# Weight quarters, weight loads and early feed-forward products move to other slots of a transformer block kernel on one Trainium2 core

## Chip, core and metric

The kernel runs on one core of a Trainium2 chip. The metric is the device time of one execution in microseconds (us); lower is better.

## What is computed

A transformer block over 16 sequences of 256 rows of 256 numbers, all fp32: self attention, cross attention against a context of 192 numbers per row, and a gated feed-forward. Cut to what matters:

```python
D_MODEL, D_COND, N_HEADS, D_HEAD = 256, 192, 16, 64
D_ATTN, D_FF = N_HEADS * D_HEAD, 4 * D_MODEL
def _attention(xq, xkv, wq, wk, wv, wo, bo):
    q, k, v = xq @ wq, xkv @ wk, xkv @ wv          # split into 16 heads of 64
    attn = softmax(q k^T * D_HEAD ** -0.5)
    return (attn v) @ wo + bo
h = _layernorm(x, ln1_g, ln1_b)
x = _attention(h, h, sa_wq, sa_wk, sa_wv, sa_wo, sa_bo) + x
h = _layernorm(x, ln2_g, ln2_b)
x = _attention(h, cond_emb, ca_wq, ca_wk, ca_wv, ca_wo, ca_bo) + x
h = _layernorm(x, ln3_g, ln3_b)
p = h @ ff_w1 + ff_b1
a, gate = p[..., :D_FF], p[..., D_FF:]
x = (a * gelu(gate)) @ ff_w2 + ff_b2 + x
```

## The kernel before

Every fp32 product is made of three rounded ones (high by high, high by low, low by high), so most operands exist as a pair high and low, and some engine splits them.

**Slots.** Attention is a software pipeline, written out by hand, of 256 slots (ATT), one for each pair of heads of each sequence: slots 0 to 127 are self attention, 128 to 255 cross attention, eight (PAIRS) for each sequence. In slot c, TensorE (PE) makes the scores of pair c (tile S, L428/L429), a projection of queries and keys for a later pair (QKB), part of a projection of values (VB), the output product of pair c-4 (WOP, L577), the transposes of the probabilities of c-1 (PTB, L539), and probabilities by values of c-2 (PVB, L597). VectorE (DVE) finds the row maxima (NM), splits QKB and the probabilities (PL), adds halves; ScalarE (ACT) does the exponentials (PT) and copies out of PSUM; GpSimd (POOL) splits values (VR), divides and splits the outputs (ON, then OT, in that order behind everything else of its slot) and splits weights. Each engine works its slots strictly in order.

**Projections.** For slots 0 to 31 (OLD) and for the last eight (LAST = 248 on) a pair is projected alone, three slots ahead (AHEAD): `pe_project`, L508. In between one product serves two sequences, keys and queries in turns, seven slots ahead (LEAD): `pe_project_both`, L526. Where both fall into one slot (c = 25 to 28, called late), the lone one comes behind the transposes. There is one bank QKB: each product waits until DVE has split the one before (L843 or L851). As the lone ones of the end start at c = 245, slots 241 to 244 have no projection, and neither have 253 to 255.

**Copies.** SyncE (SP) walks the same slots. In each turn it issues four copies of a pair's queries and keys (RX from QKS, L630 and L632, needed by the scores), one store and two loads of the softmax denominators, and what else is due: rows, x, weights. The denominators' load waits for POOL's product ON of two pairs earlier (L1498).

**Weights.** The cross-attention weights and then the feed-forward ones are staged in six chunks each: SP loads a chunk of 512 KB into STG in a sequence's first slot (pair 0). POOL splits it in four quarters (`pool_split_w`: L1019, L1021, and for the query chunks a scaling, L1017) into a ring of two places (SPL) in the pairs QUARTERS, 1, 2, 5 and 6; SP stores each quarter to DRAM one turn later (`store_split`, L1538). Split k waits until store k-2 has landed. The chunks are staged in sequences 4 to 9 and 17 to 22. Near slot 112 to 129, and again near slot 240 to 257, SP loads them into WA: for each pair of heads four transfers of 128 KB (`load_pair`, two in each of two turns), and for the values' chunks four of 256 KB per half (`load_four`).

**Feed-forward.** It has 64 steps, eight for each of eight chunks of rows: a first product (12 matmuls of 512 columns, L1184), Gelu on ACT, product and split on DVE, a second product (12 of 256 columns, L1202). The rows of the first chunk are prepared during slots 240 to 254, and steps 0 to 3 are woven into PE's slots 256 to 259.

## Time and profile before

| | us |
|---|---|
| median of 3 runs (lowest to highest) | 1746.31 (1742.96 to 1747.38) |
| the profiled execution's own time | 1743.33 |
| its span | 1741.5 |
| mean granted clock of TensorE | 0.997 |
| PE busy | 1701.8 (98%) |
| DVE, ACT, POOL busy | 1406.2, 1236.6, 1086.2 |

The span runs from the first to the last instruction of the profiled execution; its own time is 1.8 us longer. PE counts as busy from a matmul's start to its modelled end, so that short waits do not show in its share. A window is a stretch of the span, counted from its start.

### The profile page before, as it was taken

To read this page: it belongs to the slowest core of one execution; us is meant where nothing else is said; L and a number is where in the kernel's file an instruction comes from. 1 tells how busy PE (TensorE), PEld (TensorE's weight loads), DVE (VectorE), ACT (ScalarE), POOL (GpSimd) and SP (SyncE) were. 2 spreads that over 40 slices of the span, in tenths; PEclk is the share of its full clock that TensorE was granted. 3 is DMA by queue.
4 is the path that set the end of the run, shared out by engine and by line. 5 is a ranking of instruction groups with operands and counts; after the bars stand their busy time and mean duration, and the time that the engine had idled before them with its cause. 6 is when DMAs were issued, how large, how long until landed. Compare 5 with 4: busy or idle time off the path is not lost.

```text
span 1741.5 us, 39097 instructions
## 1 busy us (share of the span) xinstructions
PE 1701.8 (98%) x11712; PEld 1564.2 (90%) x11712; DVE 1406.2 (81%) x2964; ACT 1236.6 (71%) x3370; POOL 1086.2 (62%) x1812
## 2 busy tenths in 40 slices
PE   9999999999999999999999999999999999999999
PEld 8998898989999999889888899999999888888888
DVE  8897788888888888788888888888888877656664
ACT  7887777878888888778778788888888776222222
POOL 7775577767766666688777777777776555222211
PEclk9999999999999999999999999999999999999999
DMA  7775577778766677887777788776666776211210
GB/s 217 182 184 144 155 201 189 195 194 213 194 179 156 157 176 194 214 208 189 197 202 200 206 207 205 175 184 169 166 168 161 177 200 159 73 49 61 66 45 25
DMA packets 321234, 288.92 MB, mean 166 GB/s; under 512 B 104064, under 2 KB 281344, under 8 KB 321024
## 3 DMA queue, kind: packets, MB, share of 16 engines
q1 hardware_dynamic: 267232, 273.29, 60.4%
q10 hardware_dynamic: 53792, 13.12, 3.5%
q8 instruction: 96, 1.57, 0.4%
q14 instruction: 114, 0.93, 0.2%
HBM read 82.98 MB, written 37.49 MB: 69 GB/s over the span
## 4 chain that ended last, share of the span: by engine, by line
PE 64%; SPq 17%; issue 4%; DMA 4%; POOL 4%; DVE 3%; ACT 3%; ACTq 0%; POOLq 0%; DVEq 0%
PE QKB L526 9%; PE PVB L597 9%; PE PTB L539 8%; PE WOP L577 6%; PE VB L461 5%; PE PTB L1184 5%; PE S L1184 5%; SPq L632 5%; SPq L630 4%; PE S L428 4%; PE S L429 4%; SPq L1502 4%; PE QKB L1202 3%; PE VB L1202 3%; PE QKB L508 2%
## 5 line engine op out<-in xcount | busy, mean ns | idle before, releaser
L734 ACT ACTIVATE PT<-S,NM 128x256 f32<-128x256 f32 x1024 | 471.1, 472 | 193.2 <-DVE NM L862 192.5
L837 DVE TENSOR_TENSOR PL<-PTB,PH 128x512 fp32r<-128x512 f32 x512 | 350.8, 686 | 147.8 <-ACT PH L761 125.3
L1075 POOL TENSOR_TENSOR ON<-ON,RB 128x256 f32<-128x256 f32 x256 | 187.9, 734 | 283.9 <-DVE ON L882 261.4
L862 DVE TENSOR_REDUCE NM<-S 128x2 f32<-128x512 f32 x512 | 326.4, 679 | 0.4
L761 ACT ACTIVATE PH<-PTB 128x1024 fp32r<-128x1024 f32 x256 | 265.5, 1037 | 41.3 <-PE PTB L539 39.7
L539 PE MATMUL PTB<-IDN,PT 128*128 128x128 f32 x2048 | 271.3, 274 | 5.2 <-DVE PL L837 5.1
L428 PE MATMUL S<-RX 128*128 128x256 f32 x1012 | 254.9, 284 | 2.4 <-DMA RX<-QKS 1.9
L429 PE MATMUL S<-RX 128*128 128x256 f32 x1012 | 254.0, 283 | 0.0
L577 PEld LDWEIGHTS WOP<-WO,OT 128*128 128x128 f32 x1536 | 216.1, 190 | 38.7 <-POOL OT L1080 19.2
L526 PE MATMUL QKB<-HT,WA 128*128 128x512 f32 x936 | 242.4, 394 | 2.3 <-DVE QKS L843 2.0
L539 PEld LDWEIGHTS PTB<-IDN,PT 128*128 128x128 f32 x2048 | 230.0, 140 | 10.8 <-DVE PL L837 10.2
L577 PE MATMUL WOP<-WO,OT 128*128 128x256 f32 x1536 | 225.9, 283 | 13.9 <-POOL OT L1080 13.6
L882 DVE TENSOR_TENSOR ON<-PVB,ON 64x256 f32<-64x256 f32 x512 | 213.4, 417 | 3.5
L710 ACT ACTIVATE ON<-PVB 64x256 f32<-64x256 f32 x512 | 193.9, 379 | 21.9 <-PE PVB L597 5.7
L734 ACT ACTIVATION_READ_ACCUMULATOR PT<-S,NM 128x1 f32 x1024 | 207.5, 203 | 0.0
L1080 POOL TENSOR_TENSOR OT<-ON,OT 128x256 fp32r<-128x256 f32 x256 | 191.6, 748 | 20.5
L1056 POOL TENSOR_TENSOR VR<-VF,VR 128x256 fp32r<-128x256 f32 x256 | 189.2, 739 | 20.5
L428 PEld LDWEIGHTS S<-RX 128*128 128x128 f32 x1012 | 194.1, 192 | 3.8 <-DMA RX<-QKS 3.8
L429 PEld LDWEIGHTS S<-RX 128*128 128x128 f32 x1012 | 194.6, 192 | 0.0
L526 PEld LDWEIGHTS QKB<-HT,WA 128*128 128x128 f32 x936 | 165.8, 189 | 30.8 <-DVE QKS L843 2.8
L597 PE MATMUL PVB<-PH,VR 128*128 128x256 f32 x1024 | 184.1, 301 | 6.3 <-issue 5.7
L851 DVE TENSOR_TENSOR QKS<-QKB,QKS 128x512 fp32r<-128x512 f32 x216 | 149.4, 692 | 22.6 <-ACT QKS L690 9.2
(151 smaller groups left out, 2941.9 us busy)
## 6 DMA issues: line engine op xcount, KB each, us to landing
RX<-QKS SPq DMA_DIRECT2D x506, 192.0 KB, 2.9
RX<-QKS SPq DMA_DIRECT2D x506, 128.0 KB, 2.9
RB<-denominators SPq DMA_DIRECT2D x512, 64.0 KB, 2.7
weights<-SPL SPq DMA_DIRECT2D x48, 256.0 KB, 3.3
out_dram<-XR SPq DMA_DIRECT2D x32, 256.0 KB, 3.7
WA<-weights SPq DMA_DIRECT2D x64, 128.0 KB, 2.7
rows<-XN SPq DMA_DIRECT2D x24, 256.0 KB, 2.6
rows<-HF SPq DMA_DIRECT2D x23, 256.0 KB, 2.7
```

The costliest lines, as they stand in the source:

```text
L428: e.matmul(o, q, RX[:, c % 2, i, K1, :], start=True, stop=False)
L429: last = e.matmul(o, q, RX[:, c % 2, i, K2, :], start=False, stop=True)
L526: last = e.matmul(QKB[:, :], w[:, p * P:(p + 1) * P], act, start=i == 0, stop=i == len(passes) - 1)
L539: last = e.transpose(PTB[:, i, kt * S + qt * P:kt * S + (qt + 1) * P], PT[:, s % 2, q0:q0 + P], IDN[:, :])
L577: last = e.matmul(WOP[:, t * D:(t + 1) * D], OT[:, op, t * P:(t + 1) * P], WO[:, p, wp, :], start=begins(s) and t == 0 and j == 0, stop=en ...
L597: last = e.matmul(PVB[:, i * S:(i + 1) * S], VR[:, s // 2 % 2, kt, s % 2, i * P:(i + 1) * P], part[:, first:first + S], start=i == 0 and j ...
L710: last = e.activation(ON[OWN[i], s % 2, :], PVB[OTHER[i], i * S:(i + 1) * S], ACT.Copy)
L734: last = e.activation(PT[:, c % 2, j * S:(j + 1) * S], S1[:, i, qt * S:(qt + 1) * S], ACT.Exp, bias=NM[:, j:j + 1], accum_out=DEN[:, c % 2 ...
L761: e.activation(PH[:, s % 2, :], PTB[:, :, :].rearrange("p i n -> p (i n)"), ACT.Copy) \
L837: e.tensor_tensor(PL[:, cols], PTB[:, i, :], PH[:, s % 2, cols].bitcast(F32), ALU.subtract).then_inc(a.dve_pl, 1)
L862: e.tensor_reduce(NM[:, i * TT:(i + 1) * TT], S1[:, i, :].rearrange("p (t s) -> p t s", t=TT), AX.X, ALU.max, negate=True).then_inc(a.dve_ ...
L882: last = e.tensor_tensor(on, PVB[OWN[i], i * S:(i + 1) * S], on, ALU.add)
```

## The change

- POOL's quarters of the cross weights are split in the pairs 3, 4, 5 and 6 of sequences 4 to 9 (they were in 1, 2, 5, 6). Those of the feed-forward weights are split two to a sequence, in the pairs 5 and 6 (HALVES), over sequences 17 to 28, with a staging load in every second sequence. The scaling of the query weights (L1017) goes; the norm's gain and bias get the factor, once, on ACT.
- The stored quarters are counted by two semaphores, one for each place of SPL.
- `load_pair` is one transfer of 512 KB for a pair of heads, in one turn (there were four of 128 KB in two turns). `load_four` is two transfers of 512 KB per half, in every second turn (there were four of 256 KB in four turns).
- In the late slots 25 to 28 the values' product stands ahead of the joint projection.
- The last eight pairs are projected seven slots ahead (c = 241 to 248) and take other places in QKS. In slots 249 to 254 the six first products of feed-forward steps 0 to 2 (EARLY = 3) are made in QKB by the new `pe_raw`, and ACT copies them to SBUF (`act_copy_raw`, one copy each).
- The preparation of the first rows moves ten slots ahead (FFN_START = ATT - 10), its split rows lie in HT, and the later steps' splits in QKS. PE's slots 256 to 259 are woven with first products 3, 4 and 5 and second products 0 and 1.

```diff
-CROSS_LOADS = 4
+VALUE_LOADS = 2
+EARLY = 3
+RAWS = 2 * EARLY
+FFN_START = ATT - 10
 SPLIT = 4
 PIECES = ((0, 0), (1, 0), (2, 0), (0, 1), (1, 1), (0, 2), (1, 2), (2, 1), (2, 2), (0, 3), (1, 3), (2, 3))
-QUARTERS = (1, 2, 5, 6)
+QUARTERS = (3, 4, 5, 6)
+HALVES = (5, 6)
...
+    if last_alone(k):
+        return (7, 1, 2, 0, 3, 4, 5, 6)[k - LAST]
...
-            late = 0 < c < DIRECT or joint(c + LEAD) and alone(c + AHEAD)
+            late = 0 < c < DIRECT or joint(c + LEAD) and first_alone(c + AHEAD)
+            if late and joint(c + LEAD):
+                pe_value_turn(e, c)
             if joint(c + LEAD):
                 pe_project_both(e, c + LEAD)
-            if alone(c + AHEAD) and not late:
+            if first_alone(c + AHEAD) and not late:
                 pe_project(e, c + AHEAD)
-
-            if 0 <= c < ATT:
+            if last_alone(c + LEAD):
+                pe_project(e, c + LEAD)
+            if ATT <= c + LEAD < ATT + RAWS:
+                pe_raw(e, c + LEAD - ATT)
+
+            if 0 <= c < ATT and not (late and joint(c + LEAD)):
...
+            if n == B:
+                e.wait_ge(s_gain, 1)
...
-            if k > DIRECT + 1:
+            if k >= LAST:
+                held = max(m for m in range(DIRECT, k) if unit(m) == unit(k))
+                e.wait_ge(d_dup[held % 2], 16 * COPIES * copied(held))
...
             if k > 1:
-                e.wait_ge(d_ws, 16 * (k - 1))
-            if done == 0 and n < KD:
-                e.tensor_scalar(STG[:, cols], STG[:, cols], SCALE, None, ALU.mult).then_inc(s_sc, 1)
-                e.wait_ge(s_sc, k + 1)
+                e.wait_ge(d_ws[k % 2], 16 * (k // 2))
...
-            if pair in QUARTERS and B + 1 <= seq <= B + NCH:
-                pool_split_w(e, seq - B - 1, 3 + NCH + seq - B, QUARTERS.index(pair), NCH)
+            if pair in HALVES and B + 1 <= seq <= B + 2 * NCH:
+                n, half = divmod(seq - B - 1, 2)
+                pool_split_w(e, n, 4 + NCH + n, 2 * half + HALVES.index(pair), NCH)
...
-        FH = HT[:, 0, :, :, :, :].rearrange("p a k x s -> p (a k x s)") \
-            .rearrange("p (r a s) -> p r a s", r=2, a=2)
+        FH = QKF.rearrange("p (r a s) -> p r a s", r=2, a=2)
+        SPF = SPL[:, :, :, :].rearrange("p r a n -> p r (a n)").bitcast(F32)
...
+        def pe_raw(e, n):
+
+            c, g = divmod(n, 2)
+            if n == 0:
+                e.wait_ge(a.dve_lo, ATT)
+                e.wait_ge(fs.s_ht, KD)
+            else:
+                e.wait_ge(fs.act_raw, n)
+            if g == 0:
+                e.wait_ge(d_wq[c % 2], 16 * (PAIRS // 2 + c // 2 + 1))
+            i = 0
+            for k in range(KD):
+                for wp, ap in ((0, 0), (0, 1), (1, 0)):
+                    last = e.matmul(QKB[:, :], w1(k, wp, g * FF + c * P), rounded(0, ap, k), start=i == 0, stop=i == 5)
+                    i += 1
+            last.then_inc(fs.pe_raw, 1)
+
+        def act_copy_raw(e, n):
+
+            e.wait_ge(fs.pe_raw, n + 1)
+            e.activation(RAW[n], QKB[:, :], ACT.Copy).then_inc(fs.act_raw, 1)
...
-            if sl.has(c):
+            if sl.has(c) and firsts:
...
-            if sl.has(c - 1):
+            if sl.has(c - 1) and seconds:
...
-                sl.wait(e, fs.pe_f1, c + 1)
+                if c < EARLY:
+                    e.wait_ge(fs.act_raw, 2 * c + 2)
+                else:
+                    e.wait_ge(fs.pe_f1, firsts(c) + 1)
...
+                e.activation(LNG[:, 1, :, :], LNG[:, 1, :, :], ACT.Copy, scale=SCALE).then_inc(s_gain, 1)
...
-            if sl.c == ATT - 3:
-                e.wait_ge(d_dup[0], 16 * COPIES * copied(LAST - 2))
-                e.wait_ge(d_dup[1], 16 * COPIES * copied(LAST - 1))
+            if sl.c == FFN_START - 3:
+                e.wait_ge(a.pe_qk, products_of(2 * B - 4))
                 pool_ffn_hi(e, 0)
-            if sl.c == ATT - 2:
+            if sl.c == FFN_START - 2:
                 pool_ffn_hi(e, 1)
                 pool_ffn_low(e, 0)
+            if sl.c == FFN_START - 1:
                 pool_ffn_low(e, 1)
...
+            def load_pair(phase, p):
 
                 cols = slice(p * P, (p + 1) * P)
-                for n in chunks:
-                    e.dma_start(WA[:, n, :, cols].bitcast(F32), WS[phase, :, n, :, cols]).then_inc(d_wq[p % 2], 16)
+                e.dma_start(WA[:, 0:4, :, cols].bitcast(F32), WS[phase, :, 0:4, :, cols]).then_inc(d_wq[p % 2], 16)
 
             def load_four(phase, g, n):
 
-                cols = slice((2 * g + n % 2) * QW, (2 * g + n % 2 + 1) * QW)
-                e.dma_start(WA[:, 4 + n // 2, :, cols].bitcast(F32), WS[phase, :, 4 + n // 2, :, cols]) \
-                    .then_inc(d_wv[g], 16)
+                cols = slice(g * HC, (g + 1) * HC)
+                e.dma_start(WA[:, 4 + n, :, cols].bitcast(F32), WS[phase, :, 4 + n, :, cols]).then_inc(d_wv[g], 16)
 
...
-                if pair in QUARTERS and B + 1 <= seq <= B + NCH:
-                    store_split(QTR * (NCH + seq - B - 1) + QUARTERS.index(pair))
+                if pair in HALVES and B + 1 <= seq <= B + 2 * NCH:
+                    store_split(QTR * NCH + 2 * (seq - B - 1) + HALVES.index(pair))
...
+                        if phase and g:
+                            k = ATT - QUAD + i
+                            at = k - LEAD + 2
+                            freed = nth_alone(k) + 1
+                        else:
+                            j = first - 2 * PAIRS + 2 * p + 1
+                            at = j - LEAD + 3
+                            freed = nth_joint(j) + 1
+                        if c == at:
+                            await_stored(phase)
+                            e.wait_ge(a.pe_qk, freed)
+                            if p > 1:
+                                e.wait_ge(d_wq[p % 2], 16 * (PAIRS // 2 * phase + p // 2))
+                            load_pair(phase, p)
                     for g in range(2):
                         four = first - 2 * PAIRS + PAIRS * g + QUAD
...
-                        for n in range(4):
-                            if c == four + 2 + n:
-                                e.wait_ge(d_ws, 16 * QTR * NCH * (phase + 1))
+                        for n in range(2):
+                            if c == four + 2 + 2 * n:
+                                await_stored(phase)
                                 e.wait_ge(a.pe_v, tiles(four) + 2)
                                 load_four(phase, g, n)
 
...
-                if pair == 0 and B + 1 <= seq <= B + NCH:
-                    if seq == B + 1:
+                if pair == 0 and B + 1 <= seq <= B + 2 * NCH and (seq - B) % 2:
+                    n = (seq - B - 1) // 2
+                    if n == 0:
                         e.wait_ge(s_ow, 2 * PAIRS)
                     else:
-                        e.wait_ge(s_pw, QTR * (NCH + seq - B - 1))
-                    stage_ffn(seq - B - 1)
...
-            for j in range(4):
-                pe_ffn(e, Slot(j, FU, 2))
-                pe_slot(e, Slot(ATT + j, ATT))
-            ffn(e, pe_ffn, 4)
+            pe_slot(e, Slot(ATT, ATT))
+            pe_ffn(e, Slot(EARLY, FU, 2), seconds=False)
+            pe_slot(e, Slot(ATT + 1, ATT))
+            pe_ffn(e, Slot(1, FU, 2), firsts=False)
+            pe_slot(e, Slot(ATT + 2, ATT))
+            pe_ffn(e, Slot(EARLY + 1, FU, 2), seconds=False)
+            pe_ffn(e, Slot(2, FU, 2), firsts=False)
+            pe_slot(e, Slot(ATT + 3, ATT))
+            pe_ffn(e, Slot(EARLY + 2, FU, 2), seconds=False)
+            for c in range(3, EARLY + 3):
+                pe_ffn(e, Slot(c, FU, 2), firsts=False)
+            ffn(e, pe_ffn, EARLY + 3)
```

## Rows read from the trace of the kernel before

**Rows 1.** Windows of the span: busy time (matmuls) of each engine, granted clock, DMA share.
```profile
480.00:640.00 160.00, 160.00 (x1122) 149.05 (x1121) 138.40 (x296) 129.81 (x368) 103.78 (x176) 1.00 0.65 163
...
1060.00:1376.00 316.00, 314.79 (x2212) 291.38 (x2211) 278.74 (x589) 262.73 (x742) 218.26 (x371) 1.00 0.70 174
...
210.00:400.00 190.00, 184.80 (x1284) 170.30 (x1283) 157.26 (x335) 149.25 (x419) 140.41 (x237) 1.00 0.75 194
690.00:800.00 110.00, 106.79 (x728) 96.25 (x727) 91.35 (x193) 86.54 (x245) 79.97 (x139) 1.00 0.81 206
840.00:1060.00 220.00, 210.16 (x1443) 192.36 (x1442) 184.22 (x391) 171.54 (x483) 164.36 (x286) 0.98 0.79 203
1376.00:1464.00 88.00, 79.61 (x592) 71.76 (x591) 68.35 (x153) 65.92 (x191) 48.67 (x81) 1.00 0.75 194
...
855.50:858.90 3.40, 3.40 (x19) 3.40 (x18) 0.39 (x1) 1.96 (x4) 3.24 (x6) 0.50 0.81 190
```

**Rows 2.** PE's groups of matmuls between 1376 and 1464 us (busy, mean ns, idle before).
```profile
L539 PE MATMUL PTB<-IDN,PT 128*128 128x128 f32 x128 | 18.8, 277 | 4.7 <-DVE PL L837 4.6
...
L461 PE MATMUL VB<-WA,CT 128*128 128x512 f32 x31 | 9.3, 395 | 0.0
L508 PE MATMUL QKB<-HT,WA 128*128 128x256 f32 x48 | 7.1, 283 | 0.0
```

**Rows 3.** Waits between 840 and 1060 us: total us, times, longest.
```profile
POOL SPL L1019 <- DMA STG<-in_L_xattn_ff_w_dram: 21.3, 5, 5.4
...
PEld WOP L577 <- POOL OT L1080: 11.5, 7, 3.0
```

**Rows 4.** Timeline of POOL: a feed-forward quarter whose chunk lands late.
```profile
850.43 0.40 POOL L1019 CAST SPL<-STG 128x256 fp32r<-128x256 f32 x1 [4.87 <-DMA STG<-in_L_xattn_ff_w_dram]
```

**Rows 5.** Timeline of PE: the output product in the same slot.
```profile
854.34 0.97 PE L577 MATMUL WOP<-WO,OT 128*128 128x256 f32 x6 [2.04 <-POOL OT L1080]
```

**Rows 6.** Timeline of POOL: a quarter split without a wait, in a pair 5.
```profile
418.34 0.40 POOL L1019 CAST SPL<-STG 128x256 fp32r<-128x256 f32 x1
```

**Rows 7.** Timeline of SP: stores of the quarters of rows 6 and of rows 4.
```profile
427.33 0.59 SPq L1538 DMA_DIRECT2D weights<-SPL  x1
...
857.52 0.61 SPq L1538 DMA_DIRECT2D weights<-SPL  x1
```

**Rows 8.** DMA issues, whole span: size of one, median us to landing.
```profile
RX<-QKS SPq DMA_DIRECT2D x506, 192.0 KB, 2.9
...
weights<-SPL SPq DMA_DIRECT2D x48, 256.0 KB, 3.3
...
STG<-in_L_xattn_ff_w_dram SPq DMA_DIRECT2D x6, 512.0 KB, 5.8
```

**Rows 9.** Timeline of SP during the cross-weight loads, about one turn.
```profile
717.43 1.09 SPq L1545 DMA_DIRECT2D WA<-weights  x2
718.62 0.42 SPq L1550 DMA_DIRECT2D WA<-weights  x1
...
724.07 0.54 SPq L1545 DMA_DIRECT2D WA<-weights  x1
```

**Rows 10.** Waits between 690 and 800 us.
```profile
PEld S L428 <- DMA RX<-QKS: 2.8, 6, 1.1
```

**Rows 11.** Timeline of SP in a stretch without weight transfers.
```profile
1127.79 0.62 SPq L632 DMA_DIRECT2D RX<-QKS  x1
1129.25 1.10 SPq L1502 DMA_DIRECT2D RB<-denominators  x2
```

**Rows 12.** Timeline of PE: first scores of the pair whose last copy is in rows 11.
```profile
1134.94 0.28 PE L428 MATMUL S<-RX 128*128 128x256 f32 x1
```

**Rows 13.** Timeline of PE in late slot 26: the joint projection, then the lone one.
```profile
163.18 1.66 PE L526 MATMUL QKB<-HT,WA 128*128 128x512 f32 x6 [0.50 <-DVE QKS L843]
...
167.16 1.10 PE L508 MATMUL QKB<-HT,WA 128*128 128x256 f32 x7
```

**Rows 14.** Timeline of DVE in the same slot: the joint projection's split.
```profile
166.42 0.69 DVE L851 TENSOR_TENSOR QKS<-QKB,QKS 128x512 fp32r<-128x512 f32 x1
```

More of the change, by code:

```diff
@@ L68, in alone, with first_alone, last_alone @@
     return 0 <= k < OLD or LAST <= k < ATT
+def first_alone(k):
+    return 0 <= k < OLD
+def last_alone(k):
+    return LAST <= k < ATT
 def joint(j):
@@ L286, in block_kernel @@
         d_wst = sem("d_wst")
-        d_ws = sem("d_ws")
+        d_ws = [sem(f"d_ws{n}") for n in range(2)]
         d_wq = [sem(f"d_wq{n}") for n in range(2)]
@@ L700, in act_slot @@
             c = sl.c
-            late = joint(c + LEAD) and alone(c + AHEAD)
+            late = joint(c + LEAD) and first_alone(c + AHEAD)
             if sl.has(c - 3):
@@ L739, in act_slot @@
                 act_copy_qk(e, 2)
-            elif alone(c + AHEAD) and not late and not -1 <= c < DIRECT - 1:
+            elif first_alone(c + AHEAD) and not late and not -1 <= c < DIRECT - 1:
                 act_copy_qk(e, c + AHEAD)
@@ L855, in dve_slot @@
             c = sl.c
-            late = joint(c + LEAD) and alone(c + AHEAD)
+            late = joint(c + LEAD) and first_alone(c + AHEAD)
             if sl.has(c):
@@ L900, in dve_slot @@
                 dve_split_qk(e, 2)
-            elif alone(c + AHEAD) and not late and not -1 <= c < DIRECT - 1:
+            elif first_alone(c + AHEAD) and not late and not -1 <= c < DIRECT - 1:
                 dve_split_qk(e, c + AHEAD)
@@ L1094, in __init__ @@
             def __init__(self):
+                self.pe_raw = sem("pe_raw_f")
+                self.act_raw = sem("act_raw_f")
                 self.pe_f1 = sem("pe_f1_f")
@@ L1129, in gates, with firsts @@
         def gates(c, g):
-            return (QKB, VB)[g][:, :] if c == 0 else AG[c % 2][:, g, :]
+            return RAW[2 * c + g] if c < EARLY else AG[c % 2][:, g, :]
+        def firsts(c):
+            return c - EARLY
         ROWS = (XN[:, :], HF[:, :])
@@ L1221, in act_ffn_round @@
             if chunk > 1:
-                e.wait_ge(fs.pe_f1, PAIRS * (chunk - 1))
+                e.wait_ge(fs.pe_f1, firsts(PAIRS * (chunk - 1)))
             e.activation(rounded(chunk, 0, k), ROWS[k], ACT.Identity, bias=LNG[:, 2, 1, k:k + 1],
@@ L1538, in store_split, with await_stored @@
                 e.dma_start(WS[n // NCH, :, n % NCH, :, quarter * QW:(quarter + 1) * QW],
[L1539 to L1541 removed]
+                            SPL[:, k % 2, :, :].bitcast(F32)).then_inc(d_ws[k % 2], 16)
+            def await_stored(phase):
+                for done in d_ws:
+                    e.wait_ge(done, 16 * QTR // 2 * NCH * (phase + 1))
+            def load_pair(phase, p):
                 cols = slice(p * P, (p + 1) * P)
[L1544 to L1545 removed]
+                e.dma_start(WA[:, 0:4, :, cols].bitcast(F32), WS[phase, :, 0:4, :, cols]).then_inc(d_wq[p % 2], 16)
             def load_four(phase, g, n):
[L1549 to L1551 removed]
+                cols = slice(g * HC, (g + 1) * HC)
+                e.dma_start(WA[:, 4 + n, :, cols].bitcast(F32), WS[phase, :, 4 + n, :, cols]).then_inc(d_wv[g], 16)
             def fill_weights(c):
@@ L1562, in fill_weights @@
                         g, i = divmod(p, QUAD)
-                        for half in range(2):
-                            if phase and g:
-                                k = ATT - QUAD + i
-                                at = k
-                                freed = nth_alone(k) + 1
-                            else:
-                                j = first - 2 * PAIRS + 2 * p + 1
-                                at = j - LEAD + 3 + half
-                                freed = nth_joint(j) + 1
-                            if c == at:
-                                e.wait_ge(d_ws, 16 * QTR * NCH * (phase + 1))
-                                e.wait_ge(a.pe_qk, freed)
-                                if p > 1 and half == 0:
-                                    e.wait_ge(d_wq[p % 2], 16 * CROSS_LOADS * (PAIRS // 2 * phase + p // 2))
-                                load_pair(phase, p, 2 * half, 2 * half + 1)
+                        if phase and g:
[12 more added lines that the diff above has]
+                            load_pair(phase, p)
                     for g in range(2):
                         four = first - 2 * PAIRS + PAIRS * g + QUAD
-                        for n in range(4):
-                            if c == four + 2 + n:
-                                e.wait_ge(d_ws, 16 * QTR * NCH * (phase + 1))
+                        for n in range(2):
+                            if c == four + 2 + 2 * n:
+                                await_stored(phase)
                                 e.wait_ge(a.pe_v, tiles(four) + 2)
```

76 lines of the change are left out of this document (43 added, 33 removed).

## The prediction

> **What bounds the kernel now.** I read the windows of the span first. TensorE (PE) counts as busy in nearly every microsecond, so the question is only where it works slower than it can. Its matmuls can be counted: a stretch that nothing disturbs gives a pace, and what another stretch takes beyond that pace was lost there, short waits under the modelled ends of matmuls included [rows 1].
>
> The self-attention slots from 480 to 640 us take 160 us for 1122 matmuls, 0.1426 us each; the cross-attention slots from 1060 to 1376 us take 316 us for 2212, 0.1429 us each. A slot has 38 or 39 matmuls, so it takes 5.43 us (cross) or 5.56 us (self). Four stretches are slower [rows 1]:
>
> - 210 to 400 us (cross weights split on POOL): 1284 x 0.1426 = 183.1, so 6.9 us lost.
> - 690 to 800 us (cross weights loaded by SP): 728 x 0.1429 = 104.0, so 6.0 us lost.
> - 840 to 1060 us (feed-forward weights split): 1443 x 0.1429 = 206.1, so 13.9 us lost.
> - 1376 to 1464 us (the last slots). The mix differs, so I go by columns. A cross slot has 10,752 (22 matmuls of 256, 8 of 512, 8 of 128), in 5.43 us: 1,980 columns a microsecond. The 592 matmuls here are 128 of 128 columns, 32 of 512 (31 values, one feed-forward) and 432 of 256 (among them 88 of the eight lone projections, 48 of which have a row) [rows 2]: 143,360 columns, 72.4 us. So 15.6 us of 88 are lost.
>
> Together 42.4 us. The waits then name the culprits. Between 840 and 1060 us POOL waits 21.3 us in five pieces for a staged chunk, and PE waits for OT [rows 3]. The timeline shows one piece: POOL stands 4.87 us at the first quarter, and in that slot PE stands 2.04 us at the output product [rows 4, 5]. So a late POOL of up to 4.87 - 2.04 = 2.8 us is absorbed. Behind this idle piece the granted clock is 0.50 for 3.4 us, its lower level of 1.2 GHz: 1.7 us more [rows 1]. In the last slots PE's idle time before the transposes is DVE's PL [rows 2]: four slots and then three have no projection between the scores and the transposes, and without that cover DVE's maxima and split are seen.
>
> **The change part by part.**
>
> *Quarters in other pairs.* The chunk is issued in pair 0 and lands 5.8 us later (median) [rows 8], about one slot. POOL asks for it in pair 3 (three slots, 16 us) or pair 5, so this wait goes: 13.9 us in the feed-forward part, and the 6.9 us of the self part, where L1017 goes too. POOL's own work stays under a slot: it is busy 164 of 220 us with the quarters [rows 1]. There is a new wait, however. In the self part four quarters now follow in four slots, and split k needs the store of k-2 landed. From a split's start to its store's issue the timeline shows 427.33 - 418.34 = 9.0 us, and a store lands 3.3 us later [rows 6, 7, 8]: 12.3 us against two slots, 11.1 us. So POOL will stand some 1.2 us in pairs 5 and 6. Behind it in its slot are ON and OT, which the output product waits for, but 2.8 us are absorbed. And the wait limits itself: with POOL late, the issue came 857.52 - 850.43 = 7.1 us behind the split [rows 4, 7], because SP is then paced by POOL's own ON; 10.4 us in all. PE should see nothing. Bounds: 0 to 6.9 us; I take 6.5 us for the self part. The feed-forward quarters have a whole sequence between k and k+2. I leave 0.9 us for their later neighbours and take 13.0 us (bounds 9.3, if a third stays as another wait, to 13.9). The new wait for the gain's factor is for work done a hundred slots earlier: nothing.
>
> *Fewer weight transfers.* In the loading stretch one turn of SP takes 724.07 - 717.43 = 6.64 us, more than a slot of 5.43; 1.7 us of it are three weight transfers [rows 9]. The queue is the bound there, and PE's scores wait for late copies [rows 10]. Without them a turn has 0.8 us left, from 1128.41 to 1129.25 [rows 11], so its work is some 4.6 us. With pairs in odd turns and fours in even ones there is now at most one transfer in a turn, 0.55 us if the larger one costs as much to issue [rows 9]: 5.2 us, just under a slot. Rows and x transfers come on top in some turns, and the bytes are the same. So the stretch is nearly, not wholly, freed: 4.5 us of 6.0 (bounds: a loss of 13, see the rivals, to 6.0). In the last slots the same transfers are fewer too; that is in the next term but one.
>
> The Trainium skill (DMA: Bandwidth & Descriptors, Anatomy of one DMA) puts a DMA at about 2.0 us plus its bytes by 436 GB/s, given for the GpSimd path; for 512 KB that would be 3.2 us, and merging four transfers would cost almost nothing. The trace doesn't agree under this load: 5.8 us for a staged chunk of that size [rows 8]. By the page this term would be the whole 6.0 us, by the row the 4.5 us taken.
>
> *Values first in the late slots.* In slot 26 the joint projection waits 0.50 us for QKB, and the values ahead of it would fill that [rows 13]. But the lone projection starts at 167.16, 0.05 us after DVE ends the joint split at 166.42 + 0.69 [rows 13, 14]. DVE comes to this split through the maxima and ACT's exponentials of the same scores, which the order of the values doesn't touch. So the wait moves from the joint to the lone projection. I take 0; bounds 0 and 3 x 0.50 = 1.5 us.
>
> *The last slots.* Fourteen slots (241 to 254) get a projection or a raw product each, so PE's slots are full and the covers are back. Nothing is added for PE: the 36 matmuls of the raw products are taken from the feed-forward steps. The copies of a pair's queries and keys no longer hang on a projection three slots ahead; normally they have 1134.94 - 1127.79 - 2.9 = 4.2 us to spare [rows 8, 11, 12]. ACT makes six PSUM copies more, in slots where it had none of QKB to copy; DVE has no split for them. The first rows' preparation falls into slots 230 to 245, where DVE is 88% busy [rows 1], as it is while any sequence is prepared, and no other sequence is. PE's slot 255 and the four behind it stay thin: scores 255, then only outputs and transposes before the first products. Of 15.6 us I leave 3.0 for both. That is 12.6 us (bounds 6, if DVE sets half of the slots, to 15.6).
>
> Sum: 6.5 + 13.0 + 4.5 + 0 + 12.6 = 36.6 us. Against the profiled execution's own 1743.33 that is 1706.7 us. That execution lies 3.0 us under the median of the runs, so the same saving from the median gives 1709.7; I forecast 1708 us.
>
> **The rivals.**
>
> *The large load holds the copies back.* A transfer of 512 KB takes 5.8 us where one of 192 KB takes 2.9 [rows 8], and the copies of the next turn follow it in the queue. The delay of 2.9 us is under the spare 4.2 us, which speaks against; but the spare is thin where the queue is full. If each of the twelve large loads of the first phase costs the longest wait seen there, 1.1 us [rows 10], that is 13 us, and the 4.5 us aren't had: 1724 us. The Trainium skill (same page, Queues, rings and completion order) says that the descriptors of a queue are consumed in ring order, which is this rival's mechanism; no row here separates it from the issue time.
>
> *The end stays bound by DVE.* Then it gives 6 us and not 12.6: 1713 us. For it: PL ends PE's waits there. Against: the slots before 1376 us have the same DVE work and run at full pace.
>
> *The store's landing becomes the wait, and it is slower.* It decides once the lag from split to landing passes 11.1 + 2.8 = 13.9 us. At a POOL wait as long as that of rows 4, lag 16 us, each of the twelve splits in pairs 5 and 6 of the self part idles PE 2.04 us [rows 5] and draws 1.7 us of half clock [rows 1]: 12 x 3.74 = 45 us more, 1752 us, slower. Against: 12.3 and 10.4 us measured. At a lag of 15 us it is 1.1 us each, too short for the clock to fall: 13 us, 1720 us.
>
> *The waits only change names.* POOL and SP are freed, but ACT's or DVE's order sets the same pace: no change, 1746 us. Against: two long stretches without these waits run at 0.143 us a matmul.
>
> **How the numbers follow.** Forecast as such 0.70 (1699 to 1713), DVE-bound end 0.12, held copies 0.08, store's landing in its milder form 0.03 and its slower form 0.03, names only 0.04. The low end is all terms in full and the 1.5 us: 1743.3 - 42.4 - 1.5 = 1699. The high end takes in the first rival, 1724. A measurement of this kernel tells 0.3%, some 5 us. Faster 0.93, same 0.04, slower 0.03.
>
> **What would show it.** Right: no wait of POOL's quarters for the staged chunks; short waits, 1 to 2 us, for the stores in pairs 5 and 6 of sequences 4 to 9, and no PE wait for OT behind them; granted clock 1.00 throughout; from 840 to 1060 us some 1540 matmuls instead of 1443; SP's turns with weights under 5.5 us; in the late slots the 0.50 us moved to the lone projection; slots 241 to 254 of 5.4 us. Wrong: PE waiting for RX in slots 110 to 130, POOL waits above 2.8 us, or slots near 240 at 5.8 us and more with PE waiting for PL.

## The result, and the profile after

The changed kernel takes 1714.82 us (median of 4 runs, 1713.36 to 1716.02), the kernel before 1744.63 (4 runs beside them, 1742.15 to 1747.38). The ratio is 0.9828, with a 95% interval of 0.9809 to 0.9847. The forecast was 1708, range 1699 to 1724. The span went from 1741.5 to 1713.0 us, 28.5 us less, where the sum of the prediction had 36.6.

Which part gave what can be read from the starts of the slots. In each trace I take from PE's timeline where the transposes of pair n begin (PTB<-IDN,PT, L539 before, L555 after), and subtract. PE makes the transposes of pair n in its slot n+1; a stretch "slots 32 to 118", here and in the experiments, runs from the transposes of pair 32 to those of pair 118.

| stretch | before, from to | after, from to | saved | predicted |
|---|---|---|---|---|
| start to slot 32 (values first) | 0, 212.93 | 0, 213.03 | -0.1 | 0 |
| slots 32 to 118 (self quarters) | 212.93, 699.42 | 213.03, 691.98 | 7.5 | 6.5 |
| 118 to 136 (loads) | 699.42, 803.77 | 691.98, 790.04 | 6.3 | 4.5 |
| 136 to 200 (feed-forward quarters) | 803.77, 1165.40 | 790.04, 1138.12 | 13.5 | 13.0 |
| 200 to 224 | 1165.40, 1295.89 | 1138.12, 1268.66 | 0.0 | 0 |
| 224 to the end (last slots) | 1295.89, 1741.54 | 1268.66, 1712.98 | 1.3 | 12.6 |

Four terms came as large as predicted or a little larger. The largest but one, 12.6 us, gave 1.3. First the windows of the changed kernel; the columns are as in [rows 1] (window, length, PE, PEld, DVE, ACT, POOL, granted clock, DMA share, GB/s).

```profile
210.00:400.00 190.00, 190.00 (x1332) 177.05 (x1331) 162.65 (x348) 154.96 (x434) 139.69 (x239) 1.00 0.77 200
690.00:800.00 110.00, 109.34 (x768) 101.23 (x767) 96.75 (x208) 90.86 (x257) 86.34 (x149) 1.00 0.81 207
840.00:1060.00 220.00, 218.93 (x1543) 202.62 (x1541) 195.93 (x415) 183.50 (x515) 166.23 (x285) 1.00 0.79 200
...
1438.80:1442.10 3.30, 3.30 (x17) 3.26 (x15) 1.77 (x3) 1.16 (x2) 1.51 (x3) 0.50 0.48 168
1455.90:1459.20 3.30, 3.30 (x9) 2.52 (x9) 2.19 (x4) 0.00 (x0) 0.00 (x0) 0.50 0.44 137
```

The three long stretches now run at 0.1426, 0.1432 and 0.1426 us a matmul, the undisturbed pace of the two stretches in [rows 1]; before they had 1284, 728 and 1443 matmuls in the same lengths. The two short windows are new: the granted clock falls to 0.50 in PE's slot 256 and again behind slot 259, for 3.4 us each; each window lies within one such piece. Between 690 and 800 us PE no longer waits for RX [rows 10]. Between 210 and 400 us this is all that POOL's quarters wait for (total us, times, longest):

```profile
POOL SPL L1049 <- DMA weights<-SPL: 4.5, 6, 1.1
```

The wait for a staged chunk [rows 3, 4] is gone here and between 840 and 1060 us, and in its place stand six short ones for the stores. Over all 24 quarters of the self part (to 480 us) there are eight, 7.8 us in all, the longest 1.9. No PE wait for OT stands behind them.

In the late slots the timeline of PE shows the 0.50 us of [rows 13] gone and a wait in front of the lone projection instead:

```profile
163.32 1.60 PE L542 MATMUL QKB<-HT,WA 128*128 128x512 f32 x6
...
167.27 0.98 PE L524 MATMUL QKB<-HT,WA 128*128 128x256 f32 x6 [0.77 <-DVE QKS L882]
```

The tail is where the gain is missing. PE's timeline of the changed kernel in slots 255 to 259:

```profile
1434.18 0.71 PE L619 MATMUL PVB<-PH,VR 128*128 128x256 f32 x4 [0.89 <-issue]
...
1437.75 0.95 PE L599 MATMUL WOP<-WO,OT 128*128 128x256 f32 x6 [2.38 <-DVE XR L969]
...
1438.54 1.69 PE L555 MATMUL PTB<-IDN,PT 128*128 128x128 f32 x8
...
1441.73 3.13 PE L1243 MATMUL S<-HT,WA 128*128 128x512 f32 x12
...
1455.64 0.65 PE L1243 MATMUL S<-HT,WA 128*128 128x512 f32 x1 [2.05 <-DVE PT L1372]
```

PE waits 2.38 us for DVE's sum before the output product of slot 256, 0.89 us at PVB of slot 255, and 2.05 us at the first products of feed-forward step 5 (L1243). Right behind each of the two longer waits comes one of the two half-clock pieces. DVE's timeline says what it was doing before it let PE go at 1455.64:

```profile
1440.26 0.75 DVE L1372 SCALAR_TENSOR_TENSOR PT<-SPL,B,PT 128x512 f32<-128x512 f32 x1 [1.89 <-PE PTB L555]
...
1449.40 0.75 DVE L1372 SCALAR_TENSOR_TENSOR PT<-XN,B,PT 128x512 f32<-128x512 f32 x1
1450.19 0.85 DVE L1376 CAST QKS<-PT 128x512 fp32r<-128x512 f32 x1
1451.07 0.77 DVE L1378 TENSOR_TENSOR QKS<-PT,QKS 128x512 fp32r<-128x512 f32 x1
1451.77 1.57 DVE L829 TENSOR_SCALAR XN<-XR,MV,RSTD 128x256 f32<-128x256 f32 x2
1453.26 1.55 DVE L829 TENSOR_SCALAR HF<-XR,MV,RSTD 128x256 f32<-128x256 f32 x2
1454.84 0.75 DVE L1372 SCALAR_TENSOR_TENSOR PT<-S,B,PT 128x512 f32<-128x512 f32 x1
...
1461.78 0.43 DVE L1376 CAST QKS<-PT 128x512 fp32r<-128x512 f32 x1 [3.62 <-PE VB L1264]
```

Without a gap it does the product and split of an early step (L1372, L1376, L1378, 2.4 us) and the normalization of the next chunk's rows (L829, 3.1 us) and only then the product that reads S (step 3's), which first product 5 waits for, as it is made in the same bank. DVE's timeline shows no gap from 1440.26 us, behind the transposes of pair 255, to 1458.16 us.

In the kernel before, the output product of slot 256 stands behind first product 0 and doesn't wait:

```profile
1463.90 1.55 PE L1184 MATMUL QKB<-QKS,WA 128*128 128x512 f32 x6
1465.29 1.52 PE L1184 MATMUL VB<-QKS,WA 128*128 128x512 f32 x6
1466.65 0.88 PE L577 MATMUL WOP<-WO,OT 128*128 128x256 f32 x6
```

### The profile page after: what moved, and what is told of

Its sections match the earlier page's. It is cut to its first block, busy times and chain, and to the rows that moved or that the text cites. A ratio compares the mean times of both kernels' runs of the same rounds, so it can differ in the third digit from the quotient of the medians.

```text
span 1713.0 us, 39030 instructions
## 1 busy us (share of the span) xinstructions
PE 1689.9 (99%) x11712; PEld 1563.7 (91%) x11712; DVE 1407.4 (82%) x2964; ACT 1239.4 (72%) x3377; POOL 1084.6 (63%) x1804
## 3 DMA queue, kind: packets, MB, share of 16 engines
q8 instruction: 96, 1.57, 0.4%
## 4 chain that ended last, share of the span: by engine, by line
PE 89%; SPq 3%; DVE 3%; ACT 2%; issue 2%; DMA 1%; POOL 0%; ACTq 0%; DVEq 0%; POOLq 0%
PE QKB L542 16%; PE PVB L619 13%; PE PTB L555 12%; PE WOP L599 9%; PE VB L477 8%; PE S L444 6%; PE S L445 6%; PE S L1243 5%; PE PTB L1243 5%; PE QKB L1264 3%; PE VB L1264 3%; PE QKB L524 2%; ACT PT L761 1%; SPq L656 1%; SPq L654 1%
## 5 line engine op out<-in xcount | busy, mean ns | idle before, releaser
L555 PE MATMUL PTB<-IDN,PT 128*128 128x128 f32 x2048 | 268.4, 273 | 0.3 <-DVE PL L868 0.2
L555 PEld LDWEIGHTS PTB<-IDN,PT 128*128 128x128 f32 x2048 | 229.9, 140 | 3.2 <-DVE PL L868 3.0
L619 PE MATMUL PVB<-PL,VR 128*128 128x256 f32 x1024 | 163.9, 282 | 0.0
```

What stands on the lines that cost most here:

```text
L555: last = e.transpose(PTB[:, i, kt * S + qt * P:kt * S + (qt + 1) * P], PT[:, s % 2, q0:q0 + P], IDN[:, :])
L619: last = e.matmul(PVB[:, i * S:(i + 1) * S], VR[:, s // 2 % 2, kt, s % 2, i * P:(i + 1) * P], part[:, first:first + S], start=i == 0 and j ...
```

## The experiments

Each was compared with the kernel before, run on the same chip; the chips differ between some experiments, so across them I compare ratios, and stretches of the traces. "Span" is that of the profiled execution.

**1. The quarters alone.** On the kernel before:

```diff
-QUARTERS = (1, 2, 5, 6)
+QUARTERS = (3, 4, 5, 6)
+HALVES = (5, 6)
...
-            if pair in QUARTERS and B + 1 <= seq <= B + NCH:
+            if pair in HALVES and B + 1 <= seq <= B + 2 * NCH:
```

with the staging in every second sequence, two store semaphores and the gain's factor on ACT, as in the change.

> The kernel before with the quarters' part alone: splits in pairs 3 to 6 of sequences 4 to 9 and in pairs 5 and 6 of sequences 17 to 28, two store semaphores, the factor in the norm's gain. Theory (POOL's wait for the staged chunk was all that this stretch lost): it keeps the 7.5 us and the 13.5 us that the changed kernel gained there, 21 us in all, so a ratio of 0.988, and TensorE's clock is granted in full. Rival (part of that gain needs SP's queue freed by the merged loads): at most 15 us, 0.991 or more.

Measured: 1724.74 us against 1742.72, ratio 0.9893 (0.9873 to 0.9913), span 1723.9. By slot starts 6.9 us are saved up to slot 118, and 18.7 up to slot 200 and 224. The loading stretch isn't helped (118 to 136 takes 105.5 us, 1.2 more than before), 136 to 200 gains 12.9, and 1.0 us is lost again from 224 on. The window of its feed-forward quarters stands at full pace already:

```profile
840.00:1060.00 220.00, 218.83 (x1536) 202.16 (x1534) 195.91 (x415) 182.14 (x515) 164.95 (x282) 1.00 0.79 199
```

So the two quarter terms hold, each by itself.

**2. The loads alone.** On the kernel before:

```diff
-            e.wait_ge(d_wq[p % 2], 16 * CROSS_LOADS * (p // 2 + 1))
+            e.wait_ge(d_wq[p % 2], 16 * (p // 2 + 1))
...
+            def load_pair(phase, p):
+                cols = slice(p * P, (p + 1) * P)
+                e.dma_start(WA[:, 0:4, :, cols].bitcast(F32), WS[phase, :, 0:4, :, cols]).then_inc(d_wq[p % 2], 16)
...
-                        for n in range(4):
-                            if c == four + 2 + n:
+                        for n in range(2):
+                            if c == four + 2 + 2 * n:
```

> The kernel before with the merged weight loads alone. Theory (SP's queue was the bound near slots 118 to 130): about 6 us gained there; in the last slots, where four of the large loads come in four turns running, copies land late and 1 to 3 us of it go again: ratio 0.997 to 0.998. Rival (the large load holds the copies back in the first phase too): no gain, 1.000 or more.

Measured: 1732.71 against 1742.72, ratio 0.9938 (0.9918 to 0.9959), span 1731.7. That is more than either theory gave it. Slots 118 to 136 take 97.5 us (before 104.4), 6.8 us less; 136 to 200 gain 2.8 and the stretch from 224 on 2.5. The stretch from the start to slot 96 is 2.2 us slower, and I have no cause for that. The larger loads don't hold the copies back in the first phase: between 690 and 800 us PE has no wait for RX.

```profile
690.00:800.00 110.00, 109.51 (x775) 101.80 (x773) 96.02 (x204) 91.02 (x257) 84.43 (x146) 1.00 0.84 214
840.00:1060.00 220.00, 211.29 (x1460) 191.54 (x1459) 188.36 (x397) 174.62 (x494) 167.78 (x291) 1.00 0.80 206
```

775 matmuls where there were 728: with the quarters untouched, the merged loads alone take away the whole of this stretch's loss. The second window keeps most of the quarters' loss (1460, not 1540).

**3. Quarters and loads, nothing early.** Both edits; no values first, no raw products, no rows prepared early.

> The changed kernel without its last part and without the values first: quarters and merged loads, but the old last slots, no early products, first rows prepared as before. Theory (the last slots gained only 1 to 2 us, as the two traces say when their ends are compared): 1716 us, ratio 0.984. Rival, the step as predicted (12.6 us gained by the early products and lost elsewhere): 1727 us, 0.990.

Measured: 1713.63 against 1742.72, ratio 0.9831 (0.9807 to 0.9854), span 1711.3. It is as good as the whole change. So the early feed-forward products bring nothing in total, and the last stretch can be compared between the two kernels with their loads alike. Windows of this kernel, from slot 224 to 239, from there to 255, and the 38.4 us behind:

```profile
1267.90:1348.70 80.80, 80.61 (x572) 75.01 (x571) 70.05 (x147) 67.28 (x192) 54.14 (x92) 1.00 0.71 179
1348.70:1436.90 88.20, 81.03 (x605) 73.82 (x604) 70.95 (x157) 68.03 (x193) 51.30 (x85) 1.00 0.74 196
1436.90:1475.30 38.40, 38.40 (x237) 34.47 (x236) 25.07 (x48) 11.05 (x18) 16.40 (x21) 1.00 0.15 47
```

The same three windows of the changed kernel:

```profile
1268.70:1351.40 82.70, 81.97 (x572) 75.09 (x571) 73.41 (x159) 67.01 (x192) 55.29 (x94) 1.00 0.69 178
1351.40:1438.50 87.10, 82.24 (x628) 78.22 (x627) 67.49 (x145) 71.33 (x199) 49.98 (x83) 1.00 0.80 197
1438.50:1477.00 38.50, 36.45 (x212) 32.69 (x211) 26.20 (x48) 10.95 (x18) 17.47 (x21) 0.91 0.13 44
```

- 224 to 239: 1.9 us longer for the same 572 matmuls; DVE has 12 instructions and 3.4 us more (the first rows' statistics and normalization). The 1.9 us come between the transposes of pairs 231 and 237; DVE has these instructions from pair 229 to pair 236, and those of sequence 31 before them, from 223 to 226.
- 239 to 255: 1.1 us shorter, although it holds net 24 matmuls of 512 columns more (36 raw ones less the 12 of the first product 0, which the other kernel has there), 5.5 us by the 2.75 us that twelve take on the timeline. So 6.6 us of waiting are gone: the cover works.
- 255 to the end: 274.44 against 274.43 us, although it has those 24 matmuls less. So 5.5 us are lost. In 38.5 us PE does 212 matmuls instead of 237, at a clock of 0.91.

In sum 0.9 us lost (444.32 us from slot 224 to the end, against 443.44). Against the kernel before, the merged loads and the quarters bring 2.2 us from slot 224 on, and the early products take 0.9 back: the 1.3 of the table.

**4. Joint projection first in the late slots,** as before, all else changed:

```diff
-            if late and joint(c + LEAD):
-                pe_value_turn(e, c)
...
-            if 0 <= c < ATT and not (late and joint(c + LEAD)):
+            if 0 <= c < ATT:
```

> The changed kernel with the joint projection ahead of the values again in slots 25 to 28. Theory (DVE's chain sets the lone projection): slot 32's transposes start within 0.2 us of the changed kernel's 213.03 us; the joint projection waits 0.50 us again and the lone one that much less. Rival (the order earns what it fills): 1.5 to 2.0 us later.

Measured, a single run: 1715.08 us, span 1713.3, slot 32 at 212.99 (changed kernel 213.03), and the joint projection waits 0.50 us again. The order of the two is worth nothing, in either direction.

This trace shows something else. PE has the same wait of 2.38 us before slot 256's output product, but the clock stays at 1.00 behind it; only one half-clock piece is left, at step 5, so that the mean over the same 38.5 us is 0.96:

```profile
1437.69 0.95 PE L597 MATMUL WOP<-WO,OT 128*128 128x256 f32 x6 [2.38 <-DVE XR L967]
...
1438.40:1476.90 38.50, 35.09 (x210) 31.02 (x209) 26.82 (x48) 10.98 (x18) 17.41 (x21) 0.96 0.14 44
```

From slot 255 to the end it takes 274.78 us all the same, where the changed kernel with both pieces takes 274.44.

**5. The last loads one turn apart.** In the last slots of the changed kernel the pair loads come in four SP turns running, with a value load in the same turn as one of them:

```profile
RX<-QKS SPq DMA_DIRECT2D x4, 192.0 KB, 4.7
RX<-QKS SPq DMA_DIRECT2D x5, 128.0 KB, 5.2
WA<-weights SPq DMA_DIRECT2D x4, 512.0 KB, 9.5
```

These are DMA issues between 1395 and 1409 us, with the median time to landing; the profile's page has 4.6 us for the 24 large loads of the whole span and 2.9 for RX. The chain that ended last goes through one of these copies, and PEld waits 1.6 us for it at the scores of slot 251:

```profile
1401.43 7.97 DMA RX<-QKS
```

The edit puts the loads in every second turn:

```diff
-                            at = k - LEAD + 2
+                            at = ATT - 9 + 2 * i
```

> The changed kernel with the last four pair loads in every second turn (247, 249, 251, 253) instead of four turns running. Theory (the scores of slot 250 wait 1.6 us for copies that stand in the queue behind three 512 KB loads): the wait goes, landings of those loads fall from 9.5 to about 5 us, 1 to 2 us gained, 1713.5 us. Rival (that wait only covers the next one, on DVE): no gain beyond 0.5 us.

Measured: 1713.53 against 1743.33, ratio 0.9827 (0.9812 to 0.9841), span 1712.0. The wait is gone: slots 249 to 250 take 5.56 us instead of 7.25. The two loads in the same window, a pair's and a value load in the turn before, now land in 6.3 us (about 5 expected):

```profile
WA<-weights SPq DMA_DIRECT2D x2, 512.0 KB, 6.3
RX<-QKS SPq DMA_DIRECT2D x4, 192.0 KB, 4.1
```

The span is 1.0 us shorter, but half of that lies ahead of slot 224: from there to the end it is 443.87 us against 444.32. Most of the 1.7 us comes back, from slot 254 to 255 (6.93 us against 6.28) and from slot 255 to the end (275.15 against 274.44). So copies held back by large loads are real, but at one place, and cost 0.5 us, not 13. Slots 249 to 250 took 7.30 us in the kernel before too, and 6.60 in experiment 3.

**6. The normalization one step later,** so that DVE frees S for PE first (on the changed kernel):

```diff
-                if f == 2:
+                if f == (3 if chunk == 0 else 2):
...
-                if f in (4, 5):
-                    dve_ffn_turn(e, chunk + 1, f - 4)
+                first = 5 if chunk == 0 else 4
+                if f in (first, first + 1):
+                    dve_ffn_turn(e, chunk + 1, f - first)
```

> The changed kernel with the normalization of the second chunk's rows, and its turn, one feed-forward step later on DVE (for this chunk alone). Theory (behind slot 255 DVE is the bound: first product 5 waits 2.2 us for DVE's product of step 3 and the clock then falls for 3.4 us): 3.3 us of normalization leave that stretch, 2 to 4 us gained, 1711.5 us. Rival (the wait is ACT's Gelu or the bank, or the later turn stalls the next chunk): none, 1714.8 us or more.

Measured: 1716.39 against 1743.33, ratio 0.9841 (0.9826 to 0.9856), span 1712.0. No gain; the execution of the span is the fastest of the four. The wait at step 5 is gone, and PE waits 2.20 us for POOL's PH at step 8, the next chunk's first, instead. The rival holds: the later turn stalls the next chunk.

**7. Four early steps instead of three** (on the changed kernel):

```diff
-EARLY = 3
+EARLY = 4
...
-        RAW = (SPF[:, 0, :], SPF[:, 1, :], STG[:, 0:CW], STG[:, CW:2 * CW], XN[:, :], HF[:, :])
+        RAW = (SPF[:, 0, :], SPF[:, 1, :], STG[:, 0:CW], STG[:, CW:2 * CW], XN[:, :], HF[:, :],
+               VF[:, 0, :, :].rearrange("p t s -> p (t s)"), VF[:, 1, :, :].rearrange("p t s -> p (t s)"))
...
-        AG = (PTB, S1)
+        AG = (S1, PTB)
```

> The changed kernel with eight raw products (steps 0 to 3) in slots 249 to 256 instead of six; the two more are copied to VF, and the banks of the later steps change places. Theory (slots 255 and 256 lose 3.6 us because nothing stands before the output product, which waits for DVE's sum): those two waits go, and part of it comes back as DVE's backlog in the first steps; 1 to 4 us gained, 1712 us. Rival (DVE is the bound of the whole stretch): the wait moves to the first products behind slot 259, no gain.

Measured: 1717.14 against 1743.33, ratio 0.9851 (0.9835 to 0.9867), span 1715.5. Slower than the changed kernel, if anything. The 2.38 us before the output product become 1.29, but PE has less to do later and waits longer there, for the same product of DVE:

```profile
1459.59 2.93 PE L1246 MATMUL S<-HT,WA 128*128 128x512 f32 x6 [5.20 <-DVE PT L1375]
```

**8. Edits 5, 6 and 7 together.**

> The three edits together: loads spread, normalization one step later, eight raw products. Theory (three separate waits): 5 to 8 us gained on the changed kernel, 1707 to 1710 us. Rival (one bound, DVE behind slot 252): no more than the best of the three alone.

Measured: 1716.44 against 1743.33, ratio 0.9843 (0.9826 to 0.9859), span 1714.7. No gain. Three edits that each take away or shorten a wait of PE leave the end where it was: with PE's order as it is, DVE sets it.

**9. PE's order behind slot 255** (with edit 5). First product 3 goes ahead of slot 256's part, and second product 2 ahead of first product 5, so that PE has work where it waited for DVE. DVE's work stays the same:

```diff
-            pe_slot(e, Slot(ATT, ATT))
             pe_ffn(e, Slot(EARLY, FU, 2), seconds=False)
+            pe_slot(e, Slot(ATT, ATT))
...
+            pe_ffn(e, Slot(3, FU, 2), firsts=False)
             pe_ffn(e, Slot(EARLY + 2, FU, 2), seconds=False)
-            for c in range(3, EARLY + 3):
+            for c in range(4, EARLY + 3):
```

> The changed kernel with the last pair loads in every second turn, and with two products of TensorE in another place: first product 3 ahead of slot 256's output product (which waits 2.5 us for DVE's sum), second product 2 ahead of first product 5 (which waits 2.2 us for DVE). Nothing of DVE's work changes. Theory (DVE bounds the stretch behind slot 254, but TensorE's order lets it stand beside that): both covers are used, the half clock of twice 3.4 us goes with the waits, 3 to 6 us gained on the changed kernel, 1709 to 1712 us. Rival (only DVE's sum of work counts): the waits come back elsewhere in the same stretch, no more than the 1 us of the spread loads, 1713.5 us.

Measured: 1710.63 against 1743.67, ratio 0.981 (0.9793 to 0.9827), span 1708.8. From slot 224 to the end it takes 439.61 us, with edit 5 alone 443.87: 4.3 us gained. PE's timeline has S's products ahead of slot 256's outputs; one long wait is left, and the one at step 5 is down from 2.05 to 0.31 us:

```profile
1433.99 2.91 PE L1243 MATMUL S<-HT,WA 128*128 128x512 f32 x12
...
1443.16 1.19 PE L619 MATMUL PVB<-PH,VR 128*128 128x256 f32 x4 [2.90 <-DVE ON L913]
...
1454.43 0.73 PE L1243 MATMUL S<-HT,WA 128*128 128x512 f32 x2 [0.31 <-DVE PT L1372]
```

Of the two half-clock pieces one is left, around the wait of 2.90 us; I had expected both to go.

**10. The next chunk's statistics earlier** (with 9): they go to slots 250 to 252, where DVE has some room.

```diff
+            if c == ATT - 6:
+                e.wait_ge(a.dve_xo, B + HOLD + 4)
+                dve_stats(e, zero_ffn, fs, 1, 0, 1)
+            if c == ATT - 5:
+                dve_stats(e, zero_ffn, fs, 1, 2, 3)
+            if c == ATT - 4:
+                dve_aggregate(e, zero_ffn, fs, 1)
```

> e10 with DVE's statistics of the second chunk (1.8 us) made in slots 250 to 252 instead of behind slot 256. Theory (DVE's work behind slot 255 sets when first product 5 may start): another 1 to 1.8 us on e10. Rival: none.

Measured: 1710.56 against 1743.67, ratio 0.9809 (0.9792 to 0.9826), span 1708.7; 440.40 us from slot 224 on. Nothing.

**11. The first rows two slots later** (with 10): `FFN_START = ATT - 8` instead of `ATT - 10`.

> e11 with the preparation of the first chunk's rows two slots later (FFN_START = ATT - 8). Theory (slots 224 to 239 lose 1.9 us against the kernel without the early products because this preparation falls upon that of sequence 31 on DVE): 0.5 to 1.5 us come back there. Rival (DVE has no room in any full slot): the 1.9 us stay, in later slots.

Measured: 1711.05 against 1743.67, ratio 0.9816 (0.9795 to 0.9837), span 1708.2. Slots 224 to 239 take 82.75 us (with edit 5 alone 82.66). The 1.9 us of preparation stay in the stretch; they only move two slots later, as the preparation does.

Experiments 10 and 11 also tell what a half-clock piece costs behind slot 255. Both have the wait of experiment 9 (2.90 and 2.89 us); at its end a half-clock piece begins in 10 and none in 11. The first 38.5 us from slot 255 on, in 10 and then in 11:

```profile
1438.30:1476.80 38.50, 35.60 (x220) 32.42 (x219) 28.29 (x44) 11.53 (x18) 17.48 (x21) 0.96 0.15 49
...
1437.90:1476.40 38.50, 35.23 (x225) 31.83 (x225) 28.98 (x45) 11.53 (x18) 17.51 (x21) 1.00 0.17 55
```

From slot 255 to the end they take 270.35 and 270.24 us: at full clock the end comes no earlier.

**12. The second product of step 0 ahead of slot 257's part as well** (with 9):

```diff
-            pe_slot(e, Slot(ATT + 1, ATT))
             pe_ffn(e, Slot(1, FU, 2), firsts=False)
+            pe_slot(e, Slot(ATT + 1, ATT))
```

> e10 with second product 0 ahead of slot 257's two products, the second of which waits 3.1 us for DVE's split of pair 255. Theory (this wait is DVE's and can be covered): the cover is 1.4 us long, 1 to 1.5 us gained on e10, 1709.3 us, and no half clock before the end. Rival (the time comes back as a wait for first product 5): e10's 1710.6 us.

Measured: 1709.92 against 1742.84, ratio 0.9814 (0.9794 to 0.9834), span 1707.9. It can't be told from 9: the ratios overlap, from slot 224 to the end both take 439.61 us, and the 0.9 us between the spans lie ahead of slot 32. The wait of 2.90 us is gone, but PE now waits 1.58 us before the second product of step 0 and, with a half-clock piece behind it, before slot 258's output product:

```profile
1445.26 1.25 PE L599 MATMUL WOP<-WO,OT 128*128 128x256 f32 x6 [1.75 <-POOL OT L1111]
```

The best versions are 9 to 12: 1710 to 1711 us, some 4 us under the changed kernel. The runs of 9 and 12 lie between 1709.72 and 1711.35 us, the changed kernel's between 1713.36 and 1716.02, but not on the same chip, and the ratios' intervals still overlap with its own (0.9809 to 0.9847). So that they beat it is likely and not certain.

## Why the prediction was right, and where it was wrong

**What bounds the kernel.** The pace of 0.143 us a matmul as the floor, and what a stretch takes beyond it as its loss, held in three of four stretches: 48, 40 and 100 matmuls more fit into them after the change, and experiments 1 and 2 bring them in separately.

**Quarters.** Right in mechanism and size. 7.5 and 13.5 us measured, 6.5 and 13.0 predicted. The store waits came in the pairs where they were expected, but fewer and mostly shorter: eight of twelve quarters, 1.0 us in the mean and 1.9 the longest, where I had 1.2 in each. PE has no wait behind them. The rival of the store's landing is out: from a split's start to its store's landing the trace has 13.0 us at most in the self part, under the 13.9 from which PE would have seen it.

**Loads.** Right in mechanism, too small in size: 6.3 us (6.8 alone) where I took 4.5 and had 6.0 as the bound. I had put the issue of a large load at 0.55 us and left a remainder; SP's timeline shows the large ones at 0.37 to 0.56 us, no more than the small ones; that the turn is therefore free altogether is my reading of the gain. By the formula of the Trainium skill (DMA: Bandwidth & Descriptors, Anatomy of one DMA), given for the GpSimd path, 3.2 us is the estimate for 512 KB; the trace after has a median of 4.6, so the duration doesn't agree, but the stretch gained all 6 us, as by that estimate it would. My sign "SP's turns with weights under 5.5 us" failed in the last slots, where load follows load after 6.3 and 6.1 us.

**Values first.** Right: nothing. The 0.50 us moved to the lone projection (0.77 us), and experiment 4 shows that the order is worth nothing. My reason, DVE's place in its own order, fits the row, which names DVE's QKS.

**The last slots.** This is the step that failed: "Of 15.6 us I leave 3.0 for both. That is 12.6 us". Measured: 1.3, below the lower bound of 6. The cover itself works as I said, and gives 6.6 us in slots 239 to 255; PE's slots 241 to 254 take 5.38 us each in the mean, as forecast. Three things were not in the sum.

- I wrote "Nothing is added for PE: the 36 matmuls of the raw products are taken from the feed-forward steps", and counted the stretch up to slot 255 as if the 5.5 us (net) that PE no longer has to do later were gained there by themselves. They aren't: DVE's product and split of each step remain, 1.9 to 2.4 us a step, and they can't start before the transposes of pair 255 free the PT tile. From there DVE works for 17.9 us without a gap, where DVE in experiment 3's kernel has three gaps in as long a stretch, of 0.24 to 1.44 us. PE waits for it, and 24 matmuls taken from PE there shorten nothing (274.44 us against 274.43). Experiments 7 and 8 show the same: fewer products still, and PE waits 5.20 us. In the kernel before, the first product 0 stood ahead of an output product and covered DVE's sum; taking it away laid that wait bare. Experiment 9, which puts PE's products back where it waited for DVE, regains 4.3 us with DVE's work unchanged. So it is DVE's work together with PE's order that sets this stretch, not DVE's work alone.
- The first rows' preparation costs 1.9 us in slots 224 to 239, which I had at nothing on the ground that DVE does as much while any sequence is prepared.
- The pair loads in four turns running make RX late once (experiment 5: 1.7 us in one slot, 0.5 us kept to the end). As the kernel before was as slow there (7.30 us), this is a gain not had rather than a new loss.

The rival "the end stays bound by DVE" had the engine right and the mechanism not: I had it in slots 241 to 254, through PL, at 6 us; it is behind slot 255, and takes nearly all. "Granted clock 1.00 throughout" was wrong too, and 1.7 us for a half-clock piece is no price that holds everywhere. Experiment 4's trace lacks the first of the two, behind the same wait, and experiment 11's lacks the one that experiment 10's has; the end comes no earlier (274.78 us without it against 274.44, and 270.24 against 270.35). I take it that in these places PE's slower matmuls only fill time in which it would wait for DVE or POOL. The second piece, at step 5, stands in every trace that has the long wait of PE for DVE there, so its share isn't separated; DVE waits 3.62 us for PE behind it, so it may well cost its 1.7 us.

The number has luck in it. What I called the forecast as such was 1699 to 1713 us, and 1714.82 lies above it; it lies in the range because that reached to 1724 for the held copies of the first phase, which did not come. A term of 12.6 us was missed by 11.3, and the others gave 3.2 us more than taken (mostly the loads, 1.8, and the first quarters, 1.0). The forecast came within 0.4% because a miss of 11.3 us is small against 1714.

## What to carry to other kernels

A stretch's loss against an undisturbed pace of the same work, in matmuls counted per window, sizes a fix well where the fix takes away the culprit's wait: three terms came within 2 us. It fails where the fix moves work to another place: there, ask what each engine still has to do at the place it came from, and which of them ends last there; work taken from an engine that isn't the bound there comes back as waiting. And an instruction that waits for nothing may be the cover of the next one: before moving it, look at what PE would wait for if it weren't there.

## What the hardware showed that I had not expected

- The landing of a 512 KB load depends on what is queued with it far more than its issue does: 0.37 to 0.56 us on SP each time, and 4.6 us to landing in the median of 24, but 9.5 us where two go out in one turn and one in each of the turns behind it, and 6.3 us with one to a turn (experiment 5).
- The same DVE instruction took unlike times. Between 1449 and 1455 us the cast L1376 took 0.85 us, in other steps 0.43 us, and two normalizations L829 took 1.57 us. No run looked for the cause.
- A wait of PE draws the lower clock level sometimes and not always. Behind 2.04 and 2.58 us in the kernel before, and 2.38 and 2.05 us in the changed one, the granted clock is 0.50 for 3.4 us. Behind 2.15 us in the kernel before, the same 2.38 us in experiment 4 and 2.89 us in experiment 11 it stays 1.00. The shortest wait with such a piece behind it is 1.75 us (experiment 12); the start and the end of the span are left out of this.
